# Selected attention probability as the difference of two exponentials, its normalisation moved behind the value product, and the engine queues reordered, in a two-layer vision block on one core

## What is computed

```
attn = (q * scale) @ keys.T                  # 64 x 256 per head
score, index = top_k(attn, 32)               # 256 // 8
a_g = softmax(score)
out = a_g @ v[index]                         # only the 32 selected keys count
```

## Time and profile before

| | |
|---|---|
| median of 3 runs | 6441.68 us (6435.69 to 6442.96) |
| profiled execution, its own time | 6440.11 us |
| its span in the trace | 6438.2 us |
| mean granted TensorE clock | 0.73 of full |

### The profile page before, as it was taken

The page is one execution under the profiler, slowest core; times in us unless marked ns, Lnnn a source line. Parts: engine busy times, 40 slices in busy tenths (PEclk is TensorE's granted clock), DMA queues, the critical chain, the costliest instruction groups (busy, mean ns, idle before and its releaser), DMA issues.

```text
span 6438.2 us, 135940 instructions
## 1 busy us (share of the span) xinstructions
PE 4737.3 (74%) x26938; PEld 2880.6 (45%) x26938; DVE 5596.4 (87%) x24453; ACT 4054.4 (63%) x10222; POOL 4425.8 (69%) x3986
## 2 busy tenths in 40 slices
PE   3566777777777777777777777777777777777776
PEld 1333444444444444444444444444444444444444
DVE  1999999988989998999989898989999899999941
ACT  2455666666666666666666666666666666666643
POOL 1667776767677776767677677767776777777742
PEclk9666767777777777777777777777777777777777
DMA  4111111111111111111111111111111111111100
GB/s 75 39 31 42 34 40 34 40 32 42 30 41 34 39 35 34 40 32 43 32 42 30 40 36 36 38 33 40 32 43 31 43 31 32 30 30 34 33 11 10
DMA packets 585501, 229.09 MB, mean 36 GB/s; under 512 B 481152, under 2 KB 580224, under 8 KB 584576
## 3 DMA queue, kind: packets, MB, share of 16 engines
q1 hardware_dynamic: 584576, 219.25, 15.4%
HBM read 150.14 MB, written 68.80 MB: 34 GB/s over the span
## 4 chain that ended last, share of the span: by engine, by line
PE 29%; ACT 18%; issue 16%; DVE 15%; POOL 12%; ACTq 0%; DVEq 0%; POOLq 0%; DMA 0%; SPq 0%
DVE b_v L452 7%; POOL b_r L502 5%; PE y_ps L685 4%; DVE b_r L463 4%; PE h_ps L611 4%; POOL c_h L762 4%; ACT b_x L478 3%; PE a_ps L666 3%; PE pT_ps L524 3%; PE o_ps L545 2%; ACT b_e L485 2%; ACT L737 2%; PE h_ps L666 2%; POOL b_rec L493 2%; ACT L478 2%
## 5 line engine op out<-in xcount | busy, mean ns | idle before, releaser
L463 DVE MATCH_REPLACE8 b_r<-b_v,b_r 128x256 f32<-128x256 f32 x4704 | 1879.1, 416 | 0.0
L502 POOL TENSOR_SCALAR b_r<-b_r,b_rec 128x256 f32<-128x256 f32 x1568 | 1777.1, 1147 | 119.6 <-POOL b_rec L493 119.6
L452 DVE MAX8 b_v<-b_r 128x8 f32<-128x256 f32 x4704 | 1649.2, 418 | 0.0
L524 PE MATMUL pT_ps<-k_ident,b_e 128*128 128x128 f32 x3136 | 669.9, 352 | 776.3 <-ACT b_pT L532 688.3
L493 POOL TENSOR_TENSOR b_rec<-b_den,k_mone 128x4 f32<-128x4 f32 x392 | 400.5, 1022 | 1153.5 <-ACT b_x L478 1150.2
L762 POOL TENSOR_TENSOR c_h<-c_h,c_cb 128x448 f32<-128x448 f32 x672 | 760.9, 1133 | 503.9 <-ACT c_cb L739 503.0
L524 PEld LDWEIGHTS pT_ps<-k_ident,b_e 128*128 128x128 f32 x3136 | 472.6, 180 | 1161.2 <-issue 1136.2
L510 POOL TENSOR_TENSOR b_e<-b_e,b_r 128x1024 f32<-128x1024 f32 x392 | 923.5, 2356 | 18.0 <-POOL b_r L502 14.4
L685 PE MATMUL y_ps<-k_w,c_h 128*112 128x64 f32 x5376 | 776.1, 298 | 181.1 <-POOL c_h L762 177.9
L685 PEld LDWEIGHTS y_ps<-k_w,c_h 128*112 128x112 f32 x5376 | 706.5, 210 | 404.1 <-issue 403.0
L452 DVE MAX8 b_v<-b_s 128x8 f32<-128x256 f32 x1568 | 551.1, 415 | 318.0 <-POOL b_e L510 201.2
(11 more groups left out here) (146 smaller groups left out, 7904.9 us busy)
## 6 DMA issues: line engine op xcount, KB each, us to landing
q_d<-a_qe SPq DMA_DIRECT2D x56, 448.0 KB, 4.2
b_k<-k_d SPq DMA_DIRECT2D x1568, 16.0 KB, 2.0
b_v<-v_d SPq DMA_DIRECT2D x1568, 16.0 KB, 2.0
b_q<-q_d SPq DMA_DIRECT2D x392, 64.0 KB, 2.1
c_win<-vpad_d SPq DMA_DIRECT2D x56, 145.0 KB, 2.8
c_hm<-cpad_d SPq DMA_DIRECT2D x56, 145.0 KB, 2.3
vpad_d<-a_vT SPq DMA_DIRECT2D x56, 116.0 KB, 3.7
c_win<-vpad_d SPq DMA_DIRECT2D x56, 116.0 KB, 2.7
```

The costliest lines, as they stand in the source:

```text
L452: top = dve.max(out=b_v8[p][:, t, 8 * rnd:8 * rnd + 8], in_=src[:, t, :])
L463: last = dve.match_replace(out=b_r[p][:, t, :], in_to_replace=b_v8[p][:, t, 8 * rnd:8 * rnd + 8], in_values=src[:, t, :], imm_value=GONE)
L502: last = pool.tensor_scalar(out=b_r[p][:, t, :], in0=b_r[p][:, t, :], scalar1=GONE, scalar2=b_rec[p][:, t:t + 1], op0=ALU.is_le, op1=ALU.mult)
L524: last = pe.transpose(pT_ps[:, col:col + 128], b_e[p][:, t, c * 128:(c + 1) * 128], k["ident"][:, :])
```

## The change

The mask is replaced by a subtraction: exp(s - max) of all keys minus exp of the array in which the selected keys are GONE (so their exponential is 0 there) leaves the exponentials of the selected keys, exactly zero elsewhere. `act_rest` makes the second exponential in place, in two halves, `pool_prob` subtracts in two halves, and `pe_turn` waits for each half by itself. The probabilities are not normalised any more; instead four matmuls spread the inverse row sums, with the identity as the moving side, into columns 128 to 255 of the value product's PSUM tile, `act_values` copies both, and a new POOL step, NORM, multiplies the strip's values by the inverses once for each strip. The first exponentials need only the maximum and now wait for the first round of MAX8 (b_max). The queues of PE, ACT and POOL take another order inside a slot, and some places move. In `dve_select` beside what is shown only the counts of the chain semaphore change. The removed pool_mask and pool_prob are those of L495 and L506.

```diff
@@ -134,7 +134,7 @@
-        b_at = [sb(f"b_at{i}", [128, 2, RH, W]) for i in range(2)]
+        b_at = [sb(f"b_at{i}", [128, 4, RH, W]) for i in range(2)]
@@ -200,14 +200,14 @@
...
-        b_top, b_neg, b_sum, b_inv = sem("b_top"), sem("b_neg"), sem("b_sum"), sem("b_inv")
-        b_exp = sem("b_exp", 2)
-        b_msk = sem("b_msk")
-        b_prob = sem("b_prob", 2)
+        b_max, b_neg, b_sum, b_inv = sem("b_max"), sem("b_neg"), sem("b_sum", 2), sem("b_inv")
+        b_exp, b_rest = sem("b_exp", 2), sem("b_rest")
+        b_prob = sem("b_prob", 4)
...
+        b_nrm = sem("b_nrm")
...
@@ -440,82 +440,86 @@
             reg, p = tau * SLOTS + r, r % 2
             chain = b_chain
             dve.wait_ge(b_sc, reg + 2)
-            dve.wait_ge(b_prob, reg + 1)
+            dve.wait_ge(b_prob, 2 * reg + 2)
+            dve.wait_ge(b_sum, reg + 1)
...
-            last.then_inc(b_sel, 1)
+                    elif t % 2:
+                        last.then_inc(b_sel, 1)
...
+        def act_exp(act, tau, r):
             reg, p = tau * SLOTS + r, r % 2
-            act.wait_ge(b_prob, reg + 1)
-            act.wait_ge(b_top, reg + 1)
+            act.wait_ge(b_max, reg + 1)
             act.activation(b_nm[p][:, :], b_v8[p][:, :, 0], ACT.Copy, scale=-1.0).then_inc(b_neg, 1)
             act.wait_ge(b_neg, reg + 1)
+            for t in range(HP):
+                last = act.activation(b_e[p][:, t, :], b_s[p][:, t, :], ACT.Exp, bias=b_nm[p][:, t:t + 1])
+            last.then_inc(b_exp, 1)
+        def act_rest(act, tau, r):
+            reg, p = tau * SLOTS + r, r % 2
+            for half in range(2):
+                act.wait_ge(b_sel, 2 * reg + half + 1)
+                for t in range(2 * half, 2 * half + 2):
+                    last = act.activation(b_r[p][:, t, :], b_r[p][:, t, :], ACT.Exp, bias=b_nm[p][:, t:t + 1])
+                last.then_inc(b_rest, 1)
+        def act_sum(act, tau, r):
+            p = r % 2
             for t in range(HP):
                 last = act.activation(b_x8[:, t, :], b_v8[p][:, t, :], ACT.Exp, bias=b_nm[p][:, t:t + 1],
                                       accum_out=b_den[p][:, t:t + 1])
             last.then_inc(b_sum, 1)
-        def act_exp(act, tau, r):
-            p = r % 2
-            for t in range(HP):
-                last = act.activation(b_e[p][:, t, :], b_s[p][:, t, :], ACT.Exp, bias=b_nm[p][:, t:t + 1])
-            last.then_inc(b_exp, 1)
+        def pool_prob(pool, tau, r):
+            reg, p = tau * SLOTS + r, r % 2
+            for half in range(2):
+                pair = slice(2 * half, 2 * half + 2)
+                if half == 0:
+                    pool.wait_ge(b_exp, reg + 3)
+                    alone(pool)
+                pool.wait_ge(b_rest, 2 * reg + half + 1)
+                pool.tensor_tensor(out=b_e[p][:, pair, :], in0=b_e[p][:, pair, :], in1=b_r[p][:, pair, :],
+                                   op=ALU.subtract).then_inc(b_prob, 1)
         def pool_inverse(pool, tau, r):
             reg, p = tau * SLOTS + r, r % 2
-            pool.wait_ge(b_sum, reg + 1)
+            pool.wait_ge(b_sum, reg + 3)
             alone(pool)
             pool.tensor_tensor(out=b_rec[p][:, :], in0=b_den[p][:, :], in1=k["mone"][:, 0:HP], op=ALU.pow).then_inc(b_inv, 1)
-        def pool_mask(pool, tau, r):
...
-            reg, p = tau * SLOTS + r, r % 2
-            if half == 0:
-                pe.wait_ge(b_prob, reg + 3)
-                alone(pe)
+            pe.wait_ge(b_prob, 2 * reg + half + 5)
+            alone(pe)
             pe.wait_ge(b_ptc, 2 * reg + half + 1)
             alone(pe)
             for t in range(2 * half, 2 * half + 2):
@@ -536,6 +540,11 @@
             reg = tau * SLOTS + r
             pe.wait_ge(b_att, reg + 1)
             alone(pe)
+            pe.wait_ge(b_inv, reg + 1)
+            alone(pe)
+            for t in range(HP):
+                pe.matmul(o_ps[32 * t:32 * t + VH, 128:256], b_rec[r % 2][:, t:t + 1].broadcast_to([128, VH]), k["ident"][:, :],
+                          start=True, stop=True)
             for half in range(2):
                 pe.wait_ge(b_ptc, 2 * reg + half + 2)
                 alone(pe)
@@ -550,9 +559,10 @@
             reg, i, win = tau * SLOTS + r, (r // NWIN) % 2, r % NWIN
             act.wait_ge(b_pv, reg + 8)
             act.activation(b_at[i][:, :, :, win * RH:(win + 1) * RH],
-                           o_ps[:, 0:128].rearrange("c (j h q) -> c j h q", j=2, h=RH), ACT.Copy).then_inc(b_att, 1)
+                           o_ps[:, 0:256].rearrange("c (j h q) -> c j h q", j=4, h=RH), ACT.Copy).then_inc(b_att, 1)
+        NORM = 6
         UP, DOWN, TURN, TURNED, GATE, GATED, LOW, LOWED = 10, 20, 30, 31, 32, 33, 34, 35
         groups = (NE // 2, NE)
         w1, w2, b1 = (k["w1_0"], k["w1_1"]), (k["w2_0"], k["w2_1"]), (k["b1_0"], k["b1_1"])
@@ -610,7 +620,7 @@
                     for j in range(4):
                         pe.matmul(h_ps[0:C, 0:STRIP], lepe_tap[:, j, :], moving[j], start=(j == 0), stop=False)
                     pe.matmul(h_ps[0:C, 0:STRIP], lepe_tap[0:C, 4, :], c_cor[i][:], start=False, stop=False)
-                    pe.wait_ge(b_att, NWIN * (s + 1) + 1)
+                    pe.wait_ge(b_nrm, s + 1)
                     alone(pe)
                     for j in range(2):
                         last = pe.matmul(h_ps[0:C, 0:STRIP], k["att"][:, j, :], b_at[i][:, j, :, :], start=False, stop=(j == 1))
@@ -749,6 +759,9 @@
         def pool_c(pool, tau, i, step, layer):
             S, D, G = cs[layer], cb_[layer], groups[layer]
             s = tau * 2 + i
+            if step == NORM:
+                pool.wait_ge(b_att, NWIN * (s + 1) + 1)
+                pool.tensor_tensor(out=b_at[i][:, 0:2], in0=b_at[i][:, 0:2], in1=b_at[i][:, 2:4], op=ALU.mult).then_inc(b_nrm, 1)
             if step == 1:
                 pool.wait_ge(S["stat"], s + 1)
                 alone(pool)
@@ -888,15 +901,15 @@
             dve={("a", 1): 4.9, ("a", 5): 10.9, ("t", 2): 61.8,
                  ("c0", 1): 80.7, ("c0", 2): 81.7, ("c0", 3): 83.7, ("c0", 4): 85.7, ("c0", 7): 89.7,
                  ("c1", 1): 104.66, ("c1", 2): 106.66, ("c1", 3): 108.66, ("c1", 4): 109.66, ("c1", 7): 114.66},
-            pool={("a", 1): 4.9, ("c0", 1): 80.7, ("c0", 2): 81.7, ("c0", 7): 89.7, ("c0", 8): 91.7, ("c1", 1): 104.66},
+            pool={("a", 1): 4.9, ("c0", NORM): 78.2, ("c0", 1): 80.7, ("c0", 2): 81.7, ("c0", 7): 89.7, ("c0", 8): 91.7, ("c1", 1): 104.66},
             pe={("a", 3): 7.9, ("a", 4): 8.9, ("t", 1): 59.8,
-                ("c0", 0): 78.1, ("c0", TURN): 78.5, ("c0", TURNED): 78.68, ("c0", 2): 81.66, ("c0", GATE): 82.05,
-                ("c0", GATED): 82.31, ("c0", 4): 85.64, ("c0", 8): 92.3, ("c0", LOW): 92.55, ("c0", LOWED): 92.69,
+                ("c0", 0): 78.62, ("c0", TURN): 78.7, ("c0", TURNED): 78.8, ("c0", 2): 81.66, ("c0", GATE): 82.05,
+                ("c0", GATED): 82.31, ("c0", 4): 85.85, ("c0", 8): 92.3, ("c0", LOW): 92.55, ("c0", LOWED): 92.69,
                 ("c1", 0): 102.1, ("c1", TURN): 102.5, ("c1", TURNED): 102.68, ("c1", 2): 106.695, ("c1", GATE): 107.05,
                 ("c1", GATED): 107.31, ("c1", 4): 109.64},
             act={("a", 3): 7.9, ("a", 4): 8.9, ("t", 1): 59.8,
-                 ("c0", 0): 78.3, ("c0", TURN): 78.52, ("c0", 2): 81.68, ("c0", GATE): 82.12, ("c0", 3): 83.7,
-                 ("c0", 4): 85.66, ("c0", 8): 92.35, ("c0", LOW): 92.57,
+                 ("c0", 0): 78.64, ("c0", TURN): 78.72, ("c0", 2): 81.68, ("c0", GATE): 82.12, ("c0", 3): 83.7,
+                 ("c0", 4): 85.87, ("c0", 8): 92.35, ("c0", LOW): 92.57,
                  ("c1", 0): 102.3, ("c1", TURN): 102.52, ("c1", 2): 106.7, ("c1", GATE): 107.12, ("c1", 3): 108.68,
                  ("c1", 4): 109.66})
@@ -1063,18 +1076,16 @@
                         pe_scores(pe, b, 1)
                     for r in range(SLOTS):
                         before = on and (r >= 1 or not first)
-                        steps(pe, "pe", n, lo, r, fs, 0, 0.2)
                         if before:
                             pe_turn(pe, b, r - 1, 0)
                         if on and (r + 2 < SLOTS or not last):
                             pe_scores(pe, b, r + 2)
                         if before:
                             pe_turn(pe, b, r - 1, 1)
-                        steps(pe, "pe", n, lo, r, fs, 0.2, 0.4)
-                        steps(pe, "pe", n, lo, r, fs, 0.4, 0.6)
+                        steps(pe, "pe", n, lo, r, fs, 0, 0.2)
                         if before:
                             pe_values(pe, b, r - 1)
-                        steps(pe, "pe", n, lo, r, fs, 0.6, 1)
+                        steps(pe, "pe", n, lo, r, fs, 0.2, 1)
                     if last:
                         pe_turn(pe, b, SLOTS - 1, 0)
                         pe_turn(pe, b, SLOTS - 1, 1)
@@ -1091,23 +1102,25 @@
                     if first:
                         act_scores(act, b, 0)
```

(67 more changed lines are left out.)

1 line of the change is left out of this document (removed).

## The result

The changed kernel takes 6571.09 us (median of 4 runs, 6555.52 to 6602.55) against 6442.32: 1.0208 times the time over all runs, 95% interval 1.0169 to 1.0247 (the two medians alone give 1.0200). It is slower by about 129 us. The profiled execution is the slowest of the four (span 6600.8), 31 us above their median, so a difference read from its trace is up to 0.6 us per strip too large.

What follows compares the result with a forecast made beforehand. The prediction took the hand-overs between ScalarE and TensorE as the bound: 85.2 us busy plus 28.4 idle gives 113.6 per strip, 3.0 more; over 52 strips +156 on 6440.1, so 6596 us. Own range 6450 to 6690, eight-in-ten range 6230 to 6680.

Steps and rivals of the forecast that it cites:

- The change on POOL: GpSimd falls from 78 to about 49 us per strip; VectorE's 4.2 us wait for its probabilities goes.
- 105.4 us: Strip floor with selection unchanged: 110.6 less VectorE's waits of 4.2 for GpSimd and 1.0 for ScalarE's router exponential.
- ACT's busy time: ScalarE, per strip: 72.6 plus 12.6 for exponentials and value copies, 1.8 per region, gives 85.2 us.
- ACT's idle time: ScalarE's waits per strip, summed item by item along the new queues: 28.4 us, against 38.0 before.
- value product: ScalarE's wait for TensorE's value product: 5.8 us per strip before, only 1.5 left, at position 4 behind fifteen convolution matmuls.
- The new wait: Position 1: ScalarE waits 7.8 us per strip for TensorE's 8.5 us block (depthwise convolution, output projection), moved behind the value product.
- NORM: Added GpSimd product, 2.1 us per strip: free under TensorE's 6.8 us before L616, otherwise costing up to 2.1.
- DVE's gate wait: VectorE's router step at position 3 waits about 5 us for ScalarE's gate copy, giving back what GpSimd's relief won.
- By stretches: Times between ScalarE's second probability copies: positions 0-1 about 19 us, 1-2 24, 2-4 25.5, 4-6 29, remainder 16.
- signs of being right: ScalarE near 77% busy, GpSimd under 50%, a 6 to 9 us wait before the convolution copy, position 1-2 at 22 or more.
- A: Rival: VectorE becomes the bound, ScalarE-TensorE waits under 20 us per strip; 6170 us, 6080 to 6220; chance 0.14.
- B: Rival: ScalarE-TensorE chain still bounds but is shorter, idle under 25.4 us; 6315 us, 6220 to 6425; chance 0.22.

Runs made afterwards that it cites:

- before_block_under: Kernel before, mask and product kept, with the block's convolution part started at the end of slot 0, before TensorE's wait for ACT's query copies: 6188.07 us, 0.9629.
- block_first: Changed kernel with TensorE's whole block back first in slot 1, NORM in slot 0, result's copy and turn at the old places: 6554.59 us, 1.0188 to kernel before.
- before_block_late: Kernel before with only the change's late places for the block, its turn and copies, and the weights' transpose: 6579.09 us, 1.0226.
- block_under_qkv: Changed kernel, convolution started under slot 0's query copies, projection before slot 1's second transposes, NORM in slot 0, result copy and turn at old places: 6278.12 us, 0.9738.
- norm_slot0: Changed kernel with only GpSimd's NORM moved from slot 1 to slot 0: 6592.12 us, 1.0248 to the kernel before.
- conv_early: Changed kernel with the block's convolution part moved ahead of the second half's transposes in slot 1, projection left in place: 6718.21 us, 1.0427 to the kernel before.
- conv_early_norm0: Changed kernel with the convolution part ahead of the second half's transposes and NORM moved to slot 0: 6510.98 us, 1.0119 to the kernel before.
- gate_early: Changed kernel with gate matmuls and ACT's logits copy moved from the start of slots 2 and 5 to the end of slots 1 and 4: 6577.4 us, 1.0230.

## Why the prediction was right, and where not

**The sum.** Forecast 6596, +156; measured +129 between the medians, inside both ranges. The strip was to grow by 3.0 us to 113.6. Among strips with all stages it grew by 3.6, to 114.3, in the trace of the slowest run; over all those of the stretch by 3.5, to 112.5. That the sum lands so close is in part luck, since items below miss by up to 2.7 us in both directions. Its own range was also added up wrongly: +0.8 to +5.9 us per strip follow from its terms, where it says +1 to +5, and 52 times 1 and 5 on 6440 give 6492 and 6700, where it says 6450 and 6690. The result lies in either.

**The change on POOL: right** in size (43%; the subtraction took 1276 ns against "about 1.2 us", NORM 2084 against 2.1), wrong in what it was worth. "DVE's 4.2 us wait on POOL goes" came true, but the time rose all the same, and before_block_under shows that the wait goes as well without touching POOL. The 105.4 us read from those waits was the right goal with the wrong owner: before_block_under takes 105.4 us per strip over the stretch (332 regions; 105.3 among strips with all stages), with DVE busy 94%.

**ACT's busy time: 85.2 said, 82.7 found.** The exponentials took 526.8/311 = 1.69 us per region and the value copy 385 ns, both as costed; the base had been taken from two strips of 110.6 us (72.6), where the stretch has 72.3. Of the other 2.2 us, 0.6 come from counting each group to its last end: the four exponentials that start at 3089.66 last 1.69 us, but the next copy starts after 1.60, and seven times 0.09 is 0.6. The rest is not explained. (Among strips with all stages ACT is busy 83.4.)

**ACT's idle time: 28.4 said, 29.8 found.** Per strip (waits of the stretch over 44.4): the block 6.4 (7.8 said); expert products 6.2 (4.9); strip work a 5.7 (7.5), or 6.7 for each of the 38 strips that have it; short hand-overs and region scores 4.1 (5.1); value product 4.2 (1.5); transposes 2.3 (0); DVE 0.4 (0.8). The item that was missed by most is the value product, 2.7 us too small. At position 4 ACT waited 4.10 us for it in the strip read, where 3.5 of convolution and 1.1 of product against 3.1 of ACT's own work had been put. The convolution's fifteen matmuls took 5.1 us and the product 0.8, against 2.0 of ACT's own. The first nine took 3.46 us, at a granted clock of 0.53, after five microseconds at 0.50 in which TensorE was busy for 4.13:

```profile
3085.00:3090.00 5.00, 4.13 (x20) 3.32 (x21) 4.19 (x28) 2.90 (x9) 1.03 (x2) 0.50 0.16 35
3092.05:3095.51 3.46, 3.46 (x11) 1.58 (x10) 3.46 (x15) 1.96 (x10) 2.41 (x3) 0.53 0.64 127
```

In the kernel before the same nine took 1.88 us at a granted clock of 1.00, after five microseconds in which TensorE was busy throughout:

```profile
3126.43 1.88 PE L619 MATMUL h_ps<-c_hm,conv_tap 128*64 128x448 bf16 x9 [1.17 <-ACT t_a L381]
```

The levels are 1.2 and 2.4 GHz. Not every strip is like these two: over the stretch one of these matmuls has a mean of 417 ns before and 545 after, 1.2 us for the nine. The prediction had priced this convolution at its old speed, and had it begin about 2 us before ACT's last copy where it began 0.2 before (3092.05 against 3092.21).

**The new wait: right** in place and nearly in size, 6.4 us in the trace. That it alone makes the change slow holds only in part. Here are all ratios to the kernel before, by where the block stands:

| the block | old probabilities and queues | new ones |
|---|---|---|
| first in slot 1 | 1 | 1.0188 (block_first) |
| late in slot 1 | 1.0226 (before_block_late) | 1.0208 (the change) |
| begun under the query copies | 0.9629 (before_block_under) | 0.9738 (block_under_qkv) |

In the old queues the late place alone costs as much as the whole change. In the new ones the old place costs the same as the late one: ACT waits for the transposes instead, because the row sums and exponentials that it made there before now stand elsewhere. So to put the block back would not have saved the change; either step out of the kernel before costs 2%, and both together cost no more. What the four kernels of the first two rows have in common is that ACT stands behind TensorE's block, 5.14, 7.49, 5.24 and 6.78 us in the strips read. In the two of the third row it doesn't, and both are faster than the kernel before. "No cover that I can find" was wrong: TensorE waits 3.4 us for the query copies, on a PSUM tile that the block doesn't use. That gap had stood in the earlier trace rows ([3.12 <-ACT a_qe L344]).

**NORM: right and incomplete.** It costs nothing where it stands (norm_slot0). "Without that cover it would cost up to its 2.1" failed: conv_early against conv_early_norm0 shows 4.0 us per strip. TensorE's wait for it is 2.2 of them, and 1.4 the projection, which then runs at the lower clock. The sentence also left out the queue ahead of NORM, the inverse and the row sums that it waits for: they decide when NORM begins.

**DVE's gate wait: right** that it comes (6.2 us per strip, 5 said). "Gives back what it won" suggests a price. gate_early takes this wait down and the time stays, but DVE then waits nearly as long elsewhere, so that the wait has no price is not shown; it is in keeping with DVE not being the bound.

**By stretches**, one strip of the changed kernel: 0 to 1 19.6 (19 said), 1 to 2 20.7 (24), 2 to 4 27.4 (25.5), 4 to 6 29.5 (29); the remainder 14.7, or 19.7 where the loop turns (16 said, as a mean). The new wait came out shorter and 1 to 2 with it; positions 2 to 4 made up for it. Two of the signs of being right were missed: 1 to 2 was to take 22 us or more, and ACT to be busy near 77% (it is 73% of the stretch; the prediction's own 85.2 of 113.6 are 75).

**The rivals.** A and B asked for ACT's idle time under 20 or 25.4 us; it was 29.8. A's end was reached only by moving the block: DVE at 94% in block_under_qkv (6278 us) and in before_block_under, whose 6188 us lie in A's range, without any of the change.

What the new probabilities cost, together with the new order of the queues, depends on the place of the block: 1.9% with the block first (1.0188 against 1), nothing that these runs can tell with the block late (1.0208 against 1.0226), 1.1% of the kernel before with the block under the query copies (0.9738 against 0.9629). In no place do they gain. The two weren't measured apart.

## What to carry to other kernels

The engine that another one waits for can be the messenger and not the cause: before relieving it, ask what it had itself been waiting for (here POOL for ACT's row sums, and ACT for TensorE). A long piece of work on an in-order queue belongs where that engine waits for something which the piece doesn't need, and a wait that guards one buffer should stand right before the next use of that buffer. When a piece is moved, look for all that it covered: a second chain nearly as long can stand behind it.

## What the runs showed of the hardware

L247 on DVE, two inputs in SBUF, has a mean of 1188 ns in the kernel before and 505 in the changed one. The mean hides two kinds: the median is 429 and 426. In ten of the eleven strips from 1500 to 2700 us of the kernel before, one of the two falls beside POOL's product (2.06 to 2.35 us), and it ends only when the product has (1523.69 against 1523.40). The other takes 0.41 to 0.43:

```profile
1521.05 2.35 POOL L510 TENSOR_TENSOR b_e<-b_e,b_r 128x1024 f32<-128x1024 f32 x1
```

```profile
1521.49 2.20 DVE L247 TENSOR_TENSOR c_xn<-c_tok,c_mv 112x256 f32<-112x256 f32 x1
```

```profile
1577.65 0.41 DVE L247 TENSOR_TENSOR c_xn<-c_tok,c_mv 112x256 f32<-112x256 f32 x1
```

So what counts is which instruction of POOL it meets, and not how busy POOL is: with POOL at 43% the mean is 505 in the changed kernel and 823 in block_first, where NORM (2.1 us) falls beside it. It is 592 in block_under_qkv and 1134 in before_block_under, where POOL's work is the old one. L251, right behind it, also has two inputs in SBUF, and it rose from 553 to 680: together the two fell from 3.5 to 2.4 us per strip, a gain of 1.1, hidden in slack. MAX8, with one input, went only from 417 to 411, and was 411 in before_block_under too. That agrees with the rule of the Trainium skill ("SBUF — State Buffer", section "Who interferes with whom") on two SBUF inputs.
